# Gates folded into the first stage's tables, and v taken off W's later blocks by VectorE in a chunked delta rule

## The chip, the cores and the metric

One core of one Trainium2 chip runs the whole program. The metric is the device time of one execution in microseconds. The engines are named PE (matmuls; PEld is its weight load), DVE (VectorE), ACT (ScalarE), POOL (GpSimd) and SP (the queue that issues all DMAs here).

## The reference

A layer over x of 4 x 512 tokens and 512 channels, in float32: attention by a gated delta rule, a layer norm, a ternary feed-forward, a layer norm. The change lies in the delta rule, 16 heads of 128 channels:

```
q = silu(conv4(x @ Wq)); k = silu(conv4(x @ Wk)) / sqrt(128); v = silu(conv4(x @ Wv))
a = sigmoid(x @ Wa + ba)          # per head and value channel
beta = sigmoid(x @ Wb + bb)       # per head
for t in range(512):
    err = S @ k_t - v_t
    S   = a_t[:, None] * S - (beta_t * err)[:, None] * k_t[None, :]
    o_t = S @ q_t
```

## The kernel before

The program is a row of stages with barriers between them: projections (pa), recurrence (pb), attention output (pc), preparation of the feed-forward weights (pd), feed-forward (pe).

**Projections.** `projections` goes head by head through 16 heads, with the 128 channels of a head on the partitions and 2048 tokens along the free dimension. PE makes five products a head (A, V, Q, K, G, in four batches each of 12 matmuls, since each operand is split into a high and a low part). Each engine has its own `head`, in a fixed order. DVE: takes A out of PSUM into av, adds one to the exponential ra (so that ra = 1/a), multiplies -ra/128 into ng (ng then holds the gate of the error, -beta/(128 a)), and goes on with the four taps of v (L435 and three times L438), of q, `scaled_v` (v times sqrt(128) times the factors in vt, L414) and the taps of k; between them it makes the low parts of the next head's weights (`split`, L394). ACT: exponential into ra, sigmoid into av, copies of PE's banks to y, the silus. POOL multiplies products of a and 1/a inside blocks of BL = 8 tokens: factors A (inside a block, for the output), vt (to scale v), and r_out with two tables per block, the ratio of one block to the one before it and the running ratio from the chunk's start. Its steps are counted in s_pr, 21 a head. SP stores ng, A, r, vt, q, then loads the weights of the head after next, stores g and k, and loads beta for the next head into ng's buffer. ng's buffer is free for that when the store of ng has landed.

**Recurrence.** `recurrence` goes through 16 chunks of CH = 32 tokens, for 64 pairs of head and batch at once. A chunk has NBL = 4 blocks of 8 tokens; the pairs are worked on in two halves (hf 0 and 1), whose blocks alternate in an order written out by hand in `cycle` of each engine, with the numbers of banks and steps in T_... and D_... tables. PE multiplies the state UT with k and q (`state_products`); DVE's `start` scales the result by the running ratio, the first block into w (in PSUM), the later blocks into W, the q part into O. v is taken off: DVE's `first_v` for the first block, POOL's `less_v` (L778) for W's later blocks. `solve` runs 8 times a chunk: it multiplies w by the gates ng (L1188) into x and solves the block token by token (L1197, L1202). The second half's gates of blocks 2 and 3 come from ngx, a copy by ACT. x goes through ACT and PE (transposes, `cross`), and DVE's `cross` scales PE's result by the block ratio into w and adds the next block of W. POOL also multiplies pair products by the gates (`with_gates`), masks, rescales X (L799) and decays UT by crow (L771).

The lines of the diff, with the line numbers of the profile:

Of the kernel before, what the change touches and what calls it, by code (L numbers as in the profile page):

```python
# [58 lines left out]
def projections(nc, x, w_mats, ba, wb, bb, conv_w, conv_b, scr):  # L59
# [10 lines left out]
    with ExitStack() as ctx:  # L70
# [48 lines left out]
        s_st = {n: m.sem(f"st_{n}") for n in ("q", "k", "ng", "vt", "A", "g", "r")}  # L119
# [11 lines left out]
        N_PR = 21  # L131
# [68 lines left out]
        def _(pool):  # L200
# [13 lines left out]
            def head(h, first):  # L214
# [264 lines left out]
def recurrence(nc, scr, mats, wo, part, res, first):  # L479
# [17 lines left out]
    with ExitStack() as ctx:  # L497
# [238 lines left out]
        def _(pool):  # L736
# [53 lines left out]
            def cycle(c, lower, upper, p, kind):  # L790
# [359 lines left out]
        def _(dve):  # L1150
# [9 lines left out]
            def start(at, p, j, by=1):  # L1160
# [839 lines left out]
```

## Time and profile before

| | |
|---|---|
| median of 3 runs | 2785.17 us (2784.39 to 2795.73) |
| profiled execution | 2792.46 us, span 2790.7 us |
| projections | from the start to about 926 us |
| recurrence | about 932 to 2032 us |
| busy share of the span | PE 92%, PEld 79%, DVE 73%, ACT 43%, POOL 52% |
| mean granted TensorE clock | 0.968 of full speed |

A row of a timeline gives the start, the time to the end of the merged instructions, and in brackets how long the engine was idle before and for whom. A row of a group gives total busy time and the mean of one, then idle time before it by who released it. A row of waits gives total, number and longest. Matmuls are pipelined, so a busy PE need not be at its peak.

### The profile page before, as it was taken

The numbers are of one execution on the slowest core, as the hardware profiler recorded it, in microseconds if no ns is written. First come the engines' busy times: TensorE is split into PE (matmuls) and PEld (weight loads), VectorE is DVE, ScalarE is ACT, GpSimd is POOL, SyncE is SP. The second block draws the span as 40 slices with busy tenths as digits, with TensorE's granted clock in tenths as the row PEclk, the third lists the DMA queues.
The fourth block names the chain that finished last, engine by engine and source line by source line (L and its number), as shares of the span: only waits on it lengthen the run. The fifth ranks groups of instructions, "written<-read, shape, count | busy, mean of one in ns | idle before, by whom it ended". The sixth has DMA issues, their size and how long they took to land. (4 is left out here: it accounts for less than half of the span.)

```text
span 2790.7 us, 50619 instructions
## 1 busy us (share of the span) xinstructions
PE 2578.7 (92%) x17812; PEld 2216.3 (79%) x17922; DVE 2042.4 (73%) x5887; ACT 1204.5 (43%) x2393; POOL 1445.2 (52%) x1216
## 2 busy tenths in 40 slices
PE   8999999999999489999999999999749997899999
PEld 6888888888888378888888888888637776788887
DVE  4776778678769279999999999989768886433333
ACT  4445445544454233333333333323568874433333
POOL 2644553455355489999889898979422220000000
PEclk9999999999999799999999999989859999999999
DMA  5466555655664855555556566555654543100000
GB/s 132 129 177 185 150 146 163 187 143 146 171 179 124 266 201 215 200 198 198 215 227 231 214 230 227 214 197 198 240 202 158 213 188 122 67 12 11 11 11 15
DMA packets 417321, 454.39 MB, mean 163 GB/s; under 512 B 122497, under 2 KB 367233, under 8 KB 393857
## 3 DMA queue, kind: packets, MB, share of 16 engines
q1 hardware_dynamic: 417152, 452.22, 48.6%
q8 instruction: 97, 1.59, 0.2%
q14 instruction: 72, 0.58, 0.1%
HBM read 321.49 MB, written 131.14 MB: 162 GB/s over the span
## 5 line engine op out<-in xcount | busy, mean ns | idle before, releaser
L355 PE MATMUL pa_ps<-pa_x_hi,pa_w_hi 128*128 128x512 f32 x1296 | 507.0, 391 | 9.4 <-ACT pa_y L298 5.2
L355 PE MATMUL pa_ps<-pa_x_lo,pa_w_hi 128*128 128x512 f32 x1296 | 505.1, 390 | 0.0
L355 PE MATMUL pa_ps<-pa_x_hi,pa_w_lo 128*128 128x512 f32 x1296 | 504.9, 390 | 0.0
L438 DVE SCALAR_TENSOR_TENSOR pa_cv<-pa_y,pa_taps,pa_cv 128x2048 f32<-128x2048 f32 x144 | 357.1, 2480 | 17.8
L1197 DVE TENSOR_TENSOR pb_tmp<-pb_gb,pb_ps 128x112 f32<-128x112 f32 (+6 forms) x1792 | 328.5, 221 | 25.5 <-POOL pb_gb L787 11.6
L787 POOL TENSOR_TENSOR pb_gb<-pb_gb,pb_ng 128x448 f32<-128x448 f32 (+6 forms) x448 | 331.6, 786 | 2.9 <-DMA pb_gb<-scratch_pairs 2.9
L1202 DVE TENSOR_TENSOR pb_ps<-pb_ps,pb_tmp 128x112 f32<-128x112 f32 (+6 forms) x1792 | 330.8, 226 | 0.0
L355 PEld LDWEIGHTS pa_ps<-pa_x_hi,pa_w_hi 128*128 128x128 f32 x1296 | 243.6, 188 | 67.1 <-ACT pa_y L298 9.4
L771 POOL TENSOR_TENSOR all_res<-all_res,pb_crow 128x1024 f32<-128x1024 f32 x120 | 281.9, 2367 | 6.1 <-DMA pb_crow<-scratch_crow 6.1
L355 PEld LDWEIGHTS pa_ps<-pa_x_hi,pa_w_lo 128*128 128x128 f32 x1296 | 243.7, 188 | 50.7
L355 PEld LDWEIGHTS pa_ps<-pa_x_lo,pa_w_hi 128*128 128x128 f32 x1296 | 243.6, 188 | 50.0
L1033 PE MATMUL pb_ps<-pb_Gm,pb_XT 128*128 128x64 f32 (+1 forms) x2048 | 249.5, 279 | 10.0 <-DVE all_res L1222 6.3
L1033 PEld LDWEIGHTS pb_ps<-pb_Gm,pb_XT 128*128 128x128 f32 x2048 | 243.7, 197 | 16.0 <-issue 11.2
L225 POOL TENSOR_TENSOR pa_o_vt<-pa_av 128x256 f32<-128x256 f32 x16 | 11.6, 724 | 456.3 <-ACT pa_av L318 456.3
L1008 PE MATMUL pb_ps<-pb_kq,all_res 128*128 128x64 f32 x2048 | 239.6, 277 | 0.0
L1008 PEld LDWEIGHTS pb_ps<-pb_kq,all_res 128*128 128x128 f32 x2048 | 236.5, 195 | 0.7
L1891 DVE SCALAR_TENSOR_TENSOR pe_hid<-pe_ps,all_scales,pe_sil 128x512 f32<-128x512 f32 x64 | 48.1, 751 | 226.6 <-ACT pe_sil L1775 226.6
L851 ACT ACTIVATE pb_XT<-pb_ps 128x512 f32<-128x512 f32 x256 | 140.7, 595 | 137.7 <-PE pb_ps L983 137.5
L983 PEld LDWEIGHTS pb_ps<-pb_ident,pb_X 128*128 128x128 f32 x1024 | 118.5, 145 | 90.7 <-ACT pb_X L879 73.1
L983 PE MATMUL pb_ps<-pb_ident,pb_X 128*128 128x128 f32 x1024 | 144.7, 285 | 42.5 <-ACT pb_X L879 42.0
L1222 DVE TENSOR_TENSOR all_res<-all_res,pb_ps 128x512 f32<-128x512 f32 x240 | 148.7, 681 | 29.5 <-PE pb_ps L1046 29.5
L452 DVE SCALAR_TENSOR_TENSOR pa_o_ng<-pa_ra,pa_o_ng 128x512 f32<-128x512 f32 x64 | 74.5, 1222 | 127.0 <-DMA pa_o_ng<-scratch_beta 127.0
(191 smaller groups left out, 5426.9 us busy)
## 6 DMA issues: line engine op xcount, KB each, us to landing
pb_crow<-scratch_crow SPq DMA_DIRECT2D x30, 2048.0 KB, 10.0
pb_gb<-scratch_pairs SPq DMA_DIRECT2D x64, 896.0 KB, 6.6
pa_o_ng<-scratch_beta SPq DMA_DIRECT2D x16, 1024.0 KB, 7.9
scratch_ng<-pa_o_ng SPq DMA_DIRECT2D x16, 1024.0 KB, 4.5
scratch_A<-pa_o_A SPq DMA_DIRECT2D x16, 1024.0 KB, 4.5
scratch_vt<-pa_o_vt SPq DMA_DIRECT2D x16, 1024.0 KB, 4.5
scratch_q<-pa_o_q SPq DMA_DIRECT2D x16, 1024.0 KB, 6.9
scratch_g<-pa_o_g SPq DMA_DIRECT2D x16, 1024.0 KB, 7.8
```

What stands on the lines that cost most here:

```text
L355: last = nc.tensor.matmul(out, w[:, mat, k, :], xx[:, k, b * S:(b + 1) * S], start=(k == 0 and n == 0), stop=(k == KT - 1 and n == 2))
L438: nc.vector.scalar_tensor_tensor(out=out, in0=yy[:, :, k:k + S], scalar=tap(k), in1=out, op0=ALU.mult, op1=ALU.add).then_inc(s_tap, 1)
L452: last = nc.vector.scalar_tensor_tensor(out=out, in0=tile(ra, b), scalar=-1.0 / DV, in1=out, op0=ALU.mult, op1=ALU.mult)
L771: tt(uu, uu, crow[:, 8 * (e % 4):8 * (e % 4) + 8, :], ALU.mult).then_inc(s_us, 1)
L787: last = tt(pairs, pairs, ng[:, :, BL * n + t + 1:BL * (n + 1)], ALU.mult)
L851: nc.scalar.activation(out, psT[j % 2][:, :].rearrange("p (g k) -> p g k", g=4), ACT.Copy).then_inc(s_te, by)
L983: last = nc.tensor.transpose(bank[:, q * P:(q + 1) * P], src, ident[:, :])
L1008: last = nc.tensor.matmul(bank[:, 64 * q:64 * q + 64].rearrange("p (a t) -> p a t", a=2), UT[:, 8 * j + q, :], kq[p][:, :, 8 * j + q, :], ...
L1033: last = nc.tensor.matmul(bank[:, 64 * q:64 * q + 32 * kinds].rearrange("p (a i t) -> p a i t", i=4, t=BL), XT[:, g, :], Gm[:, g, 0:kinds, ...
L1197: tt(tmp[:, hs, 0:w], gb[n][:, hs, off[t]:off[t] + w], xs[:, qs, t:t + 1].broadcast_to([P, QUART, w]), ALU.mult).then_inc(s_sv, 1)
L1202: tt(xs[:, qs, t + 1:BL], xs[:, qs, t + 1:BL], tmp[:, hs, 0:w], ALU.add).then_inc(done, 1)
L1222: tt(uu, uu, tile(at, D_STATE[r] + i)[:, :].rearrange("p (q v) -> p q v", q=4), ALU.add).then_inc(s_de, 1)
```

## The change

In the projections POOL multiplies three more tables per head: vt gets the factor ng; rg is ng of blocks 1 to 3 times the ratio of the block to the one before; cg is ng times the running ratio, in ng's own buffer, once the store of ng has landed. rg is written to the memory of ra. SP stores rg and cg; the load of the next beta waits for cg's store, and ACT's exponential for rg's store. `scaled_v` waits for POOL's step 18 of now 24.

In the recurrence the gates are thus in the tables: SP loads cg into W itself and rg into its own buffer, for each half (`load_gates`). `start` multiplies by cg, `cross` by rg, `solve` has no product with gates, and ngx goes. The subtraction of v from W's later blocks goes from POOL's `less_v` to DVE's `later_v`, behind `solve(c, 0, hf)`.

```diff
 outs = {n: m.sb(f"o_{n}", [P, NCH, B, CH]) for n in ("q", "k", "ng", "vt", "A", "g")}
+outs["cg"] = outs["ng"]
+outs["rg"] = ra[:, :, :].rearrange("p b s -> p (b s)")[:, 0:TOK * (CH - BL) // CH].rearrange("p (c b t) -> p c b t", c=NCH, b=B)
...
-        N_PR = 21
+        N_PR, N_VT, N_A = 24, 18, 15
...
-                    sp.wait_ge(s_st["ng"], 16 * h)
+                    sp.wait_ge(s_st["cg"], 16 * h)
...
                 store("A")
+                store("rg")
+                store("cg")
...
+                pool.wait_ge(s_ng, h + 1)
+                mul(flat(tI), flat(tI), flat(outs["ng"]), k)
+                assert n[0] == N_VT
                 for j in range(1, NBL):
...
+                scale = lambda i: r_out[:, i, :, :, :].rearrange("p c b n -> p (c b) n").unsqueeze(3).broadcast_to([P, NCH * B, NBL, BL])
+                k = mul(by_block(outs["rg"]), by_block(outs["ng"])[:, :, 1:, :], scale(0)[:, :, 1:, :], k)
+                pool.wait_ge(s_st["ng"], 16 * h + 16)
+                mul(by_block(outs["cg"]), by_block(outs["ng"]), scale(1), k)
...
                     act.wait_ge(s_pr, N_PR * h)
+                    act.wait_ge(s_st["rg"], 16 * h)
...
-                dve.wait_ge(s_pr, N_PR * (h + 1))
+                dve.wait_ge(s_pr, N_PR * h + N_VT)
...
+            def load_gates(c, hf):
+                half = slice(HALF * hf, HALF * (hf + 1))
+                for name, dst in (("cg", W), ("rg", rg)):
+                    src = flat(scr[name][c, :, :, :]).rearrange("p (h t) -> p h t", h=HB)[:, half, :]
+                    sp.dma_start(flat(dst[:, half, :]), flat(src)).then_inc(s_gl[hf], 16)
...
                 if kind != FIRST:
+                    sp.wait_ge(s_wn[1], 6 * c)
+                    load_gates(c, 1)
...
-                sp.wait_ge(s_ngx, c + 1)
-                sp.wait_ge(s_sv, scaled(c, 3, 0))
-                sp.wait_ge(s_sv, scaled(c, 1, 1))
                 load(ng[:, :, :], "ng", c + 1, s_ngl)
+                sp.wait_ge(s_wn[0], 6 * (c + 1))
+                load_gates(c + 1, 0)
...
+            for hf in range(2):
+                load_gates(0, hf)
...
-                less_v(c, at_d - D_CH + D_S[3], 0)
...
-                less_v(c, at_d + D_S[7], 1)
...
-                nc.scalar.activation(ngx[:, :, :], ng[:, HALF:HB, CH // 2:CH], ACT.Copy).then_inc(s_ngx, 1)
...
-                tt(w_of[hf][:, 8 * q:8 * q + 8, :], src[:, :, 0, 0:BL], rr[p][:, 1, hs, 0:1].broadcast_to([P, 8, BL]), ALU.mult)
-                tt(blocks(W[:, hs, :])[:, :, 1:, :], blocks(src[:, :, 0, :])[:, :, 1:, :], cr[:, :, 1:, :], ALU.mult)
+                tt(x_of[hf][:, 8 * q:8 * q + 8, :], src[:, :, 0, 0:BL], W[:, hs, 0:BL], ALU.mult)
+                tt(W[:, hs, BL:], src[:, :, 0, BL:], W[:, hs, BL:], ALU.mult)
...
+            def later_v(at, c, hf):
+                dve.wait_ge(s_de, at + D_S[4 * hf + 3] + 1 + 4)
+                ww = W[:, HALF * hf:HALF * (hf + 1), BL:]
+                tt(ww, ww, vt[:, HALF * hf:HALF * (hf + 1), BL:], ALU.subtract).then_inc(s_wv, 1)
...
-                tt(xs, ws, gates, ALU.mult).then_inc(s_sv, 1)
...
-                    rb = groups(rr[p][:, 0, hs, n + 1:n + 2]).broadcast_to([P, 8, 4, BL])
-                    tt(groups(w_of[hf]), src[:, :, 1, :, :], rb, ALU.mult).then_inc(s_wn[hf], 1)
+                    tt(groups(x_of[hf]), src[:, :, 1, :, :], groups(rg[:, hs, BL * n:BL * (n + 1)]), ALU.mult).then_inc(s_wn[hf], 1)
...
                 solve(c, 0, 0, early=1 if kind == FIRST else 0)
+                later_v(at - D_CH, c, 0)
...
                 solve(c, 0, 1)
+                later_v(at, c, 1)
```

## Rows read from the trace of the kernel before

**Rows 1.** The page, its first part: busy time, share and instructions of each engine.
```profile
PE 2578.7 (92%) x17812; PEld 2216.3 (79%) x17922; DVE 2042.4 (73%) x5887; ACT 1204.5 (43%) x2393; POOL 1445.2 (52%) x1216
```

**Rows 2.** The table of stages: 14 heads of the projections, then 14 chunks of the recurrence.
```profile
core 0: us, PE busy (x) PEld busy (x) DVE busy (x) ACT busy (x) POOL busy (x), PEclk, DMA share, GB/s
109.00:880.00 771.00, 765.79 (x3361) 629.00 (x3360) 583.97 (x420) 376.82 (x435) 381.38 (x294) 1.00 0.57 161
1031.00:1946.00 915.00, 878.29 (x9349) 808.32 (x9446) 831.83 (x4137) 299.99 (x697) 817.61 (x735) 0.99 0.57 212
```

**Rows 3.** The waits of the same 14 heads: us in total, times, longest.
```profile
DVE pa_o_ng L452 <- DMA pa_o_ng<-scratch_beta: 124.6, 14, 9.5
...
DVE pa_ra L447 <- ACT pa_ra L316: 46.2, 14, 3.4
...
PE pa_ps L355 <- ACT pa_y L298: 5.2, 9, 0.8
```

**Rows 4.** The timeline of POOL over one head of the projections.
```profile
606.66 0.70 POOL L225 TENSOR_TENSOR pa_o_vt<-pa_av 128x256 f32<-128x256 f32 x1 [29.64 <-ACT pa_av L318]
...
627.90 4.48 POOL L225 TENSOR_TENSOR pa_r_out<-pa_r_out 128x64 f32<-128x64 f32 x3
632.33 2.44 POOL L256 COPY pa_r_out<-pa_r_out 128x64 f32<-128x64 f32 x1
661.91 0.70 POOL L225 TENSOR_TENSOR pa_o_vt<-pa_av 128x256 f32<-128x256 f32 x1 [27.15 <-ACT pa_av L318]
```

**Rows 5.** The timeline of DVE over the same head.
```profile
613.89 4.44 DVE L452 SCALAR_TENSOR_TENSOR pa_o_ng<-pa_ra,pa_o_ng 128x512 f32<-128x512 f32 x4 [9.36 <-DMA pa_o_ng<-scratch_beta]
...
651.23 1.28 DVE L394 TENSOR_TENSOR pa_w_lo<-pa_w_in,pa_w_hi 128x512 fp32r<-128x512 f32 x2
...
668.44 4.41 DVE L452 SCALAR_TENSOR_TENSOR pa_o_ng<-pa_ra,pa_o_ng 128x512 f32<-128x512 f32 x4 [8.66 <-DMA pa_o_ng<-scratch_beta]
```

**Rows 6.** The timeline of SP's queue over the end of that head.
```profile
652.69 0.40 SPq L161 DMA_DIRECT2D pa_w_in<-in_Wa  x1
...
660.61 2.37 SPq L166 DMA_DIRECT2D pa_o_ng<-scratch_beta  x1
```

**Rows 7.** The timeline of DVE in the recurrence: a gate product, its successor, start tile 7.
```profile
1511.14 0.43 DVE L1188 TENSOR_TENSOR pb_ps<-pb_ps,pb_ng 128x256 f32<-128x256 f32 x1
1511.68 0.45 DVE L1197 TENSOR_TENSOR pb_tmp<-pb_gb,pb_ps 128x112 f32<-128x112 f32 x2
...
1518.43 0.23 DVE L1166 TENSOR_TENSOR pb_ps<-pb_ps,pb_rr 128x64 f32<-128x64 f32 x1 [0.57 <-PE pb_ps L1008]
```

**Rows 8.** Two lines of the attention output: duration ns min/median/max, first and last start us.
```profile
L1402 POOL TENSOR_TENSOR pc_o_in<-pc_o_in,pc_a_in x8: 4494/4613/4787, 2044.5 to 2291.5; 128x2048 f32<-128x2048 f32 x8
...
L1569 DVE TENSOR_TENSOR pc_wo_lo<-all_res,pc_wo_hi x16: 677/684/5021, 2042.5 to 2066.5; 128x512 fp32r<-128x512 f32 x16
```

**Rows 9.** Groups of POOL in the recurrence, shapes kept apart: busy us, mean ns.
```profile
L771 POOL TENSOR_TENSOR all_res<-all_res,pb_crow 128x1024 f32<-128x1024 f32 x112 | 263.2, 2367 | 0.0
...
L778 POOL TENSOR_TENSOR pb_W<-pb_W,first_A 128x768 f32<-128x768 f32 x29 | 52.8, 1821 | 0.0
...
L799 POOL TENSOR_TENSOR pb_X<-pb_X,pb_rr 128x768 f32<-128x768 f32 x29 | 44.5, 1535 | 17.4 <-PE pb_ps L983 17.4
...
L799 POOL TENSOR_TENSOR pb_X<-pb_X,pb_rr 128x256 f32<-128x256 f32 x29 | 19.5, 672 | 64.7 <-PE pb_ps L983 64.7
```

**Rows 10.** Two lines of DVE in the projections, by duration as in rows 8.
```profile
L452 DVE SCALAR_TENSOR_TENSOR pa_o_ng<-pa_ra,pa_o_ng x64: 684/1182/1622, 51.8 to 886.1; 128x512 f32<-128x512 f32 x64
...
L438 DVE SCALAR_TENSOR_TENSOR pa_cv<-pa_y,pa_taps,pa_cv x144: 2350/2352/3106, 61.6 to 921.5; 128x2048 f32<-128x2048 f32 x144
```

**Rows 11.** The table of stages for two short stretches: stores of r, then of vt and q.
```profile
639.20:642.60 3.40, 3.40 (x16) 2.81 (x15) 3.40 (x7) 2.97 (x2) 0.00 (x0) 1.00 0.76 61
645.00:650.00 5.00, 5.00 (x24) 4.14 (x23) 4.72 (x3) 1.71 (x2) 0.00 (x0) 1.00 1.07 324
```

**Rows 12.** The timeline of ACT: the exponential of the head that POOL starts at 661.91.
```profile
656.60 1.92 ACT L316 ACTIVATE pa_ra<-pa_av 128x2048 f32<-128x2048 f32 x1
```

More of the change, by code:

```diff
@@ L118, in projections @@
         s_vt = m.sem("vt")
-        s_st = {n: m.sem(f"st_{n}") for n in ("q", "k", "ng", "vt", "A", "g", "r")}
+        s_st = {n: m.sem(f"st_{n}") for n in ("q", "k", "ng", "vt", "A", "g", "r", "rg", "cg")}
         x_rows = x.rearrange("b (s p) d -> (b s) p d", p=P)
@@ L206, in _ @@
             nc.gpsimd.memset(r_out[:, :, :, :, :], 0.0).then_inc(s_g, 4)
+            flat = lambda t: t[:, :, :, :].rearrange("p c b t -> p (c b t)")
+            by_block = lambda t: t[:, :, :, :].rearrange("p c b (n i) -> p (c b) n i", i=BL)
             at = lambda t, i: t[:, :, :].rearrange("p b (c n i) -> p i b c n", n=NBL, i=BL)[:, i]
@@ L255, in head @@
                     k = mul(rv[:, 1, :, :, j:j + 1], before, rv[:, 0, :, :, j:j + 1], k)
-                step(nc.gpsimd.tensor_copy(rv[:, 1, :, :, 0:1], rv[:, 0, :, :, 0:1]))
+                k = step(nc.gpsimd.tensor_copy(rv[:, 1, :, :, 0:1], rv[:, 0, :, :, 0:1]))
+                scale = lambda i: r_out[:, i, :, :, :].rearrange("p c b n -> p (c b) n").unsqueeze(3).broadcast_to([P, NCH * B, NBL, BL])
+                k = mul(by_block(outs["rg"]), by_block(outs["ng"])[:, :, 1:, :], scale(0)[:, :, 1:, :], k)
+                pool.wait_ge(s_st["ng"], 16 * h + 16)
+                mul(by_block(outs["cg"]), by_block(outs["ng"]), scale(1), k)
                 assert n[0] == N_PR
@@ L513, in recurrence @@
         gb = [m.sb(f"gb{i}", [P, HB, PAIRS]) for i in range(NBL)]
-        ngx = m.sb("ngx", [P, HALF, CH // 2])
+        rg = m.sb("rg", [P, HB, CH - BL])
         tmp = m.sb("tmp", [P, HB, BL - 1])
@@ L519, in recurrence @@
         psT, psD, wx = ps[0:2], ps[2:6], ps[6:8]
-        w_of = [t[:, 0:HALF * BL].rearrange("p (h t) -> p h t", t=BL) for t in wx]
-        x_of = [t[:, HALF * BL:2 * HALF * BL].rearrange("p (h t) -> p h t", t=BL) for t in wx]
+        x_of = [t[:, 0:HALF * BL].rearrange("p (h t) -> p h t", t=BL) for t in wx]
         s_id = m.sem("id")
@@ L546, in recurrence @@
         s_sv = m.sem("sv")
-        s_ngx = m.sem("ngx")
+        s_gl = [m.sem(f"gl{i}") for i in range(2)]
         s_rs = [m.sem(f"rs{i}") for i in range(2)]
@@ L1179, in solve @@
                     dve.wait_ge(s_w, 2 * c + hf + 1)
-                    dve.wait_ge(s_ngl, 16 * (c + 1))
                 else:
                     dve.wait_ge(s_wn[hf], 6 * c + 2 * n)
-                gates = ng[:, HALF * hf:HALF * (hf + 1), BL * n:BL * (n + 1)]
-                if hf and n >= NBL // 2:
-                    dve.wait_ge(s_ngx, c + 1)
-                    gates = ngx[:, :, BL * n - CH // 2:BL * (n + 1) - CH // 2]
-                ws, xs = w_of[hf], x_of[hf]
-                tt(xs, ws, gates, ALU.mult).then_inc(s_sv, 1)
+                xs = x_of[hf]
                 dve.wait_ge(s_m, NBL * c + n + 1)
-                dve.wait_ge(s_sv, 27 * k + 1)
                 quarters = [(q, slice(QUART * q, QUART * (q + 1)), slice(QUART * (2 * hf + q), QUART * (2 * hf + q + 1))) for q in range(2)]
@@ L1195, in solve @@
                         if t:
-                            dve.wait_ge(s_sv, 27 * k + 1 + 4 * (t - 1) + 2 + q + 1)
+                            dve.wait_ge(s_sv, 26 * k + 4 * (t - 1) + 2 + q + 1)
                         tt(tmp[:, hs, 0:w], gb[n][:, hs, off[t]:off[t] + w], xs[:, qs, t:t + 1].broadcast_to([P, QUART, w]),
@@ L1199, in solve @@
                     for q, qs, hs in quarters:
-                        dve.wait_ge(s_sv, 27 * k + 1 + 4 * t + q + 1)
+                        dve.wait_ge(s_sv, 26 * k + 4 * t + q + 1)
                         done = s_sv if w > 1 else s_x[hf]
@@ L1215, in cross @@
                     dve.wait_ge(s_wv, 2 * c + hf + 1)
-                    tt(w_of[hf], w_of[hf], W[:, hs, BL * (n + 1):BL * (n + 2)], ALU.add).then_inc(s_wn[hf], 1)
+                    tt(x_of[hf], x_of[hf], W[:, hs, BL * (n + 1):BL * (n + 2)], ALU.add).then_inc(s_wn[hf], 1)
             def state(at, c, r):
@@ L1238, in cycle @@
                 solve(c, 2, 0)
+                dve.wait_ge(s_gl[1], 32 * (c + 1))
                 for j in range(4, 8):
@@ L1256, in cycle @@
                     dve.wait_ge(s_os[1 - p], 16 * upper + 16 * (1 - p))
+                    dve.wait_ge(s_gl[0], 32 * (c + 2))
                     for j in range(4):
@@ L1261, in _ @@
             dve.wait_ge(s_rl[0], 32)
+            dve.wait_ge(s_gl[0], 32)
             for j in range(4):
@@ L1955, in layer @@
 def layer(nc, x, Wq, Wk, Wv, Wa, ba, Wb, bb, Wg, Wo, cqw, cqb, ckw, ckb, cvw, cvb, ln_w, ln_b, W_up, W_gate, W_down, out):
-    scr = {n: nc.dram_tensor(f"scratch_{n}", (NCH, P, NH, CT), F32, kind="Internal").ap() for n in ("q", "k", "ng", "vt", "A", "g", "o")}
+    scr = {n: nc.dram_tensor(f"scratch_{n}", (NCH, P, NH, CT), F32, kind="Internal").ap() for n in ("q", "k", "ng", "vt", "A", "g", "o", "cg")}
+    scr["rg"] = nc.dram_tensor("scratch_rg", (NCH, P, NH, B * (CH - BL)), F32, kind="Internal").ap()
     scr["beta"] = nc.dram_tensor("scratch_beta", (NH, TOK), F32, kind="Internal").ap()
```

11 lines of the change are left out of this document (1 added, 10 removed).

## Prediction

> **What bounds the kernel now.** I read the page first, then a table of stages, the waits and the timelines of one head and of one chunk. The page gives PE 92% of the span, DVE 73%, POOL 52% [rows 1]. That is an average over stages, and the diff touches two: the projections (16 heads) and the recurrence (16 chunks). In 14 heads PE is busy for 765.8 of 771 us, DVE for 584, POOL for 381; in the recurrence PE for 878 of 915, DVE for 832, POOL for 818 [rows 2].
>
> A first reading of the projections is "PE is full, the rest has room". The waits say something else. DVE never waits for PE there. It waits 124.6 us in 14 heads, 8.9 a head, for beta to land in ng's buffer, and 46.2 for the exponential, while PE waits only 5.2 us for ACT [rows 3]. One head takes 55.25 us by POOL's timeline (606.66 to 661.91) [rows 4]. The same number comes out of a loop without PE: DVE works from 613.89, when beta is there, to the end of the taps of k at 651.23 (37.3 us, where its `split` of G starts), and the next beta is there at 668.44, 17.2 us later [rows 5]; together 54.6. Those 17.2 us are fixed by SP's order: weights at 652.69 (after the split of G), g, k, then beta at 660.61 [rows 6]. PE's 240 products of a head need at most 54.7 us (3361 of them are recorded in 765.8 busy us [rows 2]). So two loops of equal length stand side by side, and whatever lengthens DVE's work between beta and the taps of k lengthens the head in full.
>
> In the recurrence DVE and PE hand over to each other: PE has 2.6 us a chunk left (36.7 over some 14 chunks), DVE still waits for PE in places (0.57 us ahead of a start tile) [rows 2, 7]. POOL is 89% busy, but nobody waits for it there.
>
> **Projections: what POOL gets.** Per head three multiplications are added, all with SBUF on both sides: v's factors by ng (128x2048), rg (128x1536, one operand broadcast), cg (128x2048, one operand broadcast). The first costs 4.6 us: the 128x2048 product of the later stage takes 4613 ns [rows 8]. For a broadcast operand the nearest rows are X by rr: 128x256 672 ns, 128x768 1535 ns, so 1.69 ns an element: 2.8 us for rg, 3.7 us for cg [rows 9]. Sum 11.1 us; at the price without broadcast (2.25 ns an element) it would be 12.7. POOL stands idle for 27 us a head [rows 4], so POOL itself takes them in: 28.1 + 11.1 us of 55.
>
> **What they do to DVE.** This decides. In the projections POOL's work runs against DVE's: a product of 128x64 there is part of a group of 3 that takes 4.48 us, and a copy of 128x64 takes 2.44 us, the length of one DVE tap [rows 4, 10]; DVE's multiplication for ng takes 684 ns at best and 1182 at the median, its taps 2350 and up to 3106 [rows 10]. Each holds the other up for one instruction, so short POOL operations cost DVE little. A long one is seen once: of 16 splits of Wo that take 684 ns at the median, one takes 5021 ns, and it runs while POOL's 4.6 us product does [rows 8]. DVE thus lost 4.34 us to an operation of 4.61, all but 0.3 of it. I take that as the price: each added operation holds DVE up for its own length less 0.3 us. All three come behind ng in POOL's order, so they fall into DVE's stretch of taps, splits and `scaled_v`: POOL's first two r_out products end at 627.9 [rows 4], DVE has work until 651. DVE's idle stretches (beta, exponential) are no refuge, because ng must exist first. So 11.1 - 3 x 0.3 = 10.2 us a head. Bounds: 0, if the one long instance does not carry over, and 12.7 at the dearer product.
>
> The Trainium skill, SBUF — State Buffer, section "Who interferes with whom", states this as a rule: a DVE instruction with two SBUF inputs contends with a GpSimd instruction that reads SBUF, the pair is held for the whole instruction and the loser blocks. By the rule DVE would lose 11.1 us a head instead of 10.2, 14 us more in all; the 5021 ns row agrees with it but for 0.3 us.
>
> **The stores and waits.** SP gets rg and cg (0.75 and 1 MB) behind the wait for POOL's last step, which moves from 634.8 to about 652 in that frame, and with them A, r, v and q move too. `scaled_v` waits only for POOL's step 18, so that is no new stall. The queue then moves A, rg, cg, r, v, q (5 MB) in a row: at 324 GB/s [rows 11], and some 4.5 us for r, whose stretch moves 61 GB/s at 0.76 busy [rows 11], that is 20 us. Weights, g, k and beta queue behind. POOL's end lies 11 to 16 us ahead of DVE's last tap, so the queue is 4 to 8 us in arrears at first; but a later beta lets POOL's short operations run alone and end earlier, which gives part back. I take 2.5 us a head, with bounds 0 and 7. The other new waits cost nothing: ACT's exponential waits for rg's store (landed some 7 us after POOL's end, A and rg at 324 GB/s and a round trip; DVE's last tap alone lies 11 us or more after that end, and without that cover it would cost up to those 7), and beta's load waits for cg's store, which lies far ahead of k in the same queue. Adding it up: 12.7 us a head, x 16 = 203 us.
>
> **Recurrence: what DVE loses and gets.** The multiplication by the gates ahead of each solve goes: start to start 0.54 us (1511.14 to 1511.68) [rows 7], 8 a chunk, 4.3 us. `start` and `cross` keep their instructions with another operand, at the same price. `later_v` adds two subtractions of 128x768 with both inputs in SBUF: 684 ns for 512 columns [rows 8] gives 1.0 us each. They are the only such instructions of DVE there, so they could hit a POOL operation (2.4 us at most, the decay of UT by crow [rows 9]). But they stand right behind each half's first solve, where POOL waits for the transposes of that solve; I take no wait, and 2.4 us each as the bound. Net -2.3 us of DVE a chunk. What of it reaches the end is less: DVE's wait for start tile 7 grows by what solve 2 saves, since PE runs without a gap from the cross product to that tile; the same holds ahead of tile 3. Following the chunk through, each half keeps 0.3 to 0.5 us: 0.8 us a chunk, -13 us over 16; bounds -37 and +38 (both subtractions behind a decay). POOL loses 2 x 1.82 us [rows 9] and ACT the copy of ngx, neither on the path. The gate loads (1.75 MB a chunk) come half a chunk before their use at a busy share of 0.57 [rows 2]; hidden.
>
> **Ends.** After the last head rg and cg are stored behind a later POOL end: +4 us. At the start of the recurrence 1.75 MB more go ahead of the gram writes, 5 us at 350 GB/s, half hidden by PE's wait for POOL's memset: +3 us.
>
> Sum: 203 - 13 + 7 = 197. The profiled execution took 2792.46 us, 7.3 above the median of the runs; against its own time 2989, against the median **2982 us**.
>
> **Rivals.**
> - *Blocked in full and queue in arrears* (the forecast): 2982, alone between 2920 and 3070. Chance 0.66.
> - *POOL's idle 27 us take it all*: long operations do not hold DVE up, heads stay at 55.25, and the recurrence gains. 2785 - 13 + 7 = 2779, and 2755 if the whole -2.3 us a chunk arrives. For it: POOL's large reserve, and a single long instance against it. It decides when the lock costs DVE under 0.4 us a head. 0.10 (half of it below -0.5%).
> - *Half of it*: DVE and POOL fall into a phase in which one or two of the three operations lie in DVE's waits, or only POOL's own loop counts (28 + 11 + three waits for a DVE tap, the store of rg 7 us, exponential and sigmoid 5.3 [rows 4, 12], some 58 us a head). 3 to 7 us a head, 2830 to 2890. 0.16.
> - *The queue dominates*: late weights hold up ACT's splits and so PE too; 18 us a head or more, 3075 and above. 0.08.
>
> About 0.5%, 14 us, can be told from no change. Faster by more 0.05, within 0.06 (the other half of the second case and little of the third), slower 0.89. The range 2850 to 3070 leaves out the second case, a part of the third and the fourth.
>
> **What would show it.** In 14 heads DVE's busy time rises by some 10 us a head while its number of instructions stays; single taps and splits of up to 5 to 7 us appear; POOL's idle time before a head shrinks to about 17 to 27 us while the head takes about 68; PE waits for ACT's copies for some 12 us a head. In the recurrence L1188 is gone, `later_v` takes 1.0 us, the waits of DVE for PE grow. It is wrong if taps stay at 2.35 us beside a 4.6 us product, or if the head's length stays at 55.

## The result, and the profile after

The changed kernel takes 2971.16 us (median of 4 runs, 2969.15 to 2979.24), the kernel before 2787.78 beside it (2784.39 to 2795.73): ratio 1.0659, 95% interval 1.0627 to 1.0691. The forecast was 2982. The profiled execution took 2972.48 us, span 2970.7, mean granted clock 0.941.

The page's busy line, as [rows 1]:

```profile
PE 2624.3 (88%) x17812; PEld 2253.6 (76%) x17922; DVE 2156.1 (73%) x5791; ACT 1197.3 (40%) x2377; POOL 1585.8 (53%) x1232
```

PE fell from 92% to 88%, and no other engine took the lead. The table of stages says where, for some 14 heads and some 14 chunks (us; PE, PEld, DVE, ACT, POOL; clock, DMA share, GB/s), as [rows 2]:

```profile
112.00:1048.00 936.00, 819.49 (x3376) 663.97 (x3375) 709.60 (x424) 382.38 (x438) 552.45 (x336) 0.93 0.59 163
1220.00:2120.00 900.00, 861.03 (x9329) 801.64 (x9425) 807.88 (x4046) 291.29 (x671) 765.09 (x703) 0.99 0.65 243
```

Some fourteen heads take 936 us instead of 771 (the windows do not begin at the same point of a head; counted between loads of beta, below, 14 heads are 937 and 777). POOL's busy time grew by 12.2 us a head ((552.45 - 381.38) / 14), the work it was given. DVE's grew by 9.0 ((709.60 - 583.97) / 14) for nearly the same instructions (424 and 420). Which of them, a view of DVE's groups tells, first of the kernel before over its 14 heads (109 to 880), then of the one after (112 to 1048); total busy us and the mean of one, idle time before it:

```profile
L438 DVE SCALAR_TENSOR_TENSOR pa_cv<-pa_y,pa_taps,pa_cv 128x2048 f32<-128x2048 f32 x126 | 309.2, 2454 | 17.2
L435 DVE TENSOR_SCALAR pa_cv<-pa_y,pa_taps,pa_cbias 128x2048 f32<-128x2048 f32 x42 | 69.1, 1645 | 0.0
...
L394 DVE TENSOR_TENSOR pa_w_lo<-pa_w_in,pa_w_hi 128x512 fp32r<-128x512 f32 x70 | 58.7, 855 | 0.0
...
L414 DVE SCALAR_TENSOR_TENSOR pa_o_vt<-pa_cv,pa_o_vt 128x512 f32<-128x512 f32 x56 | 34.9, 685 | 0.2 <-POOL pa_r_out L256 0.2
```

```profile
L452 DVE SCALAR_TENSOR_TENSOR pa_cv<-pa_y,pa_taps,pa_cv 128x2048 f32<-128x2048 f32 x126 | 339.9, 2698 | 17.2
L449 DVE TENSOR_SCALAR pa_cv<-pa_y,pa_taps,pa_cbias 128x2048 f32<-128x2048 f32 x42 | 117.8, 2804 | 0.0
L408 DVE TENSOR_TENSOR pa_w_lo<-pa_w_in,pa_w_hi 128x512 fp32r<-128x512 f32 x70 | 81.3, 1177 | 0.0
L466 DVE SCALAR_TENSOR_TENSOR pa_o_ng<-pa_ra,pa_o_ng 128x512 f32<-128x512 f32 x56 | 64.7, 1213 | 158.1 <-DMA pa_o_ng<-scratch_beta 158.1
L428 DVE SCALAR_TENSOR_TENSOR pa_o_vt<-pa_cv,pa_o_vt 128x512 f32<-128x512 f32 x56 | 58.1, 1096 | 0.0
```

The counts are equal here and the durations are not: +30.7, +48.7, +22.6 and +23.2 us in these four groups, and -2.2 in ng (66.9 before). That is 123.0 us, 8.8 a head. The wait for beta grew from 124.6 [rows 3] to 158.1, 2.4 a head. Together 11.2, of the 11.4 by which a head is longer (below).

One head shows how an instruction comes to be long. POOL's three products (L231 here), with their neighbours:

```profile
743.85 4.94 POOL L231 TENSOR_TENSOR pa_o_vt<-pa_o_vt,pa_o_ng 128x2048 f32<-128x2048 f32 x1
...
757.56 3.22 POOL L231 TENSOR_TENSOR pa_ra<-pa_o_ng,pa_r_out 128x1536 f32<-128x1536 f32 x1
760.85 4.10 POOL L231 TENSOR_TENSOR pa_o_ng<-pa_o_ng,pa_r_out 128x2048 f32<-128x2048 f32 x1
```

DVE in the same stretch:

```profile
744.23 5.64 DVE L449 TENSOR_SCALAR pa_cv<-pa_y,pa_taps,pa_cbias 128x2048 f32<-128x2048 f32 x1
...
757.94 8.76 DVE L428 SCALAR_TENSOR_TENSOR pa_o_vt<-pa_cv,pa_o_vt 128x512 f32<-128x512 f32 x4
766.63 1.34 DVE L449 TENSOR_SCALAR pa_cv<-pa_y,pa_taps,pa_cbias 128x2048 f32<-128x2048 f32 x1
```

The first tap of q takes 5.64 us beside the 4.9 us product; the first tap of k, with POOL idle, takes 1.34 us (766.63): 4.3 us lost. The four parts of `scaled_v` start 0.4 us behind rg and take 8.76 us, where four take 2.49 with POOL idle: 6.3 us lost to rg and cg (7.3 us). In sum 10.6 of 12.3 us in this head. All three products by duration (min/median/max ns):

```profile
L231 POOL TENSOR_TENSOR pa_o_vt<-pa_o_vt,pa_o_ng x16: 4612/4930/6627, 87.3 to 1070.5; 128x2048 f32<-128x2048 f32 x16
L231 POOL TENSOR_TENSOR pa_ra<-pa_o_ng,pa_r_out x16: 3199/3216/5024, 94.6 to 1085.6; 128x1536 f32<-128x1536 f32 x16
L231 POOL TENSOR_TENSOR pa_o_ng<-pa_o_ng,pa_r_out x16: 4067/4622/5736, 98.0 to 1088.9; 128x2048 f32<-128x2048 f32 x16
```

At their shortest they take 4.6, 3.2 and 4.1 us. The up to 2 us more I read as POOL waiting out an instruction of DVE first.

**Two loops take turns.** Two successive heads of DVE, from ng to ng:

```profile
663.97 5.06 DVE L466 SCALAR_TENSOR_TENSOR pa_o_ng<-pa_ra,pa_o_ng 128x512 f32<-128x512 f32 x4 [12.77 <-DMA pa_o_ng<-scratch_beta]
...
727.03 4.55 DVE L466 SCALAR_TENSOR_TENSOR pa_o_ng<-pa_ra,pa_o_ng 128x512 f32<-128x512 f32 x4 [8.49 <-DMA pa_o_ng<-scratch_beta]
...
797.00 4.78 DVE L466 SCALAR_TENSOR_TENSOR pa_o_ng<-pa_ra,pa_o_ng 128x512 f32<-128x512 f32 x4 [13.03 <-DMA pa_o_ng<-scratch_beta]
```

The first takes 63.1 us: 45.6 to the split of G (709.58), at which SP has been waiting, and 17.4 to the next ng, the 17.2 of before. The second takes 70.0 us. There POOL's last product ends at 764.95, and SP's queue runs from there to the next beta:

```profile
764.98 0.37 SPq L172 DMA_DIRECT2D scratch_A<-pa_o_A  x1
...
788.77 2.25 SPq L168 DMA_DIRECT2D pa_o_ng<-scratch_beta  x1
```

Between these two it goes from one transfer to the next without a wait (A, rg, cg, r, v, q, weights, g, k, beta): 37.9 us from ng to POOL's end, 32.0 from there to the next ng. SP's own waits for DVE's split count the heads of the first kind:

```profile
SPq L163 <- DVE pa_w_lo L408: 46.9, 7, 6.8
```

7 of 14; before it was 13 of 13 in such a window, 100.8 us. In the first head ng comes late, so POOL's short products run while DVE stands idle (POOL waits 0.70 us for ng), and POOL ends 26.9 us behind ng; beta then comes earlier, the short products run against DVE's, and POOL ends late in the next.

The three products cost DVE the same in both kinds. In the first head the 4.90 us product starts at 669.19, rg at 682.88, cg at 686.18, and DVE beside them:

```profile
669.56 5.62 DVE L449 TENSOR_SCALAR pa_cv<-pa_y,pa_taps,pa_cbias 128x2048 f32<-128x2048 f32 x1
...
683.27 3.91 DVE L449 TENSOR_SCALAR pa_cv<-pa_y,pa_taps,pa_cbias 128x2048 f32<-128x2048 f32 x1
687.32 10.61 DVE L452 SCALAR_TENSOR_TENSOR pa_cv<-pa_y,pa_taps,pa_cv 128x2048 f32<-128x2048 f32 x3
```

A first tap takes 1.34 us and three taps 7.33 with POOL idle, so 4.3, 2.6 and 3.3 us are lost, 10.1 in all, against 10.6 in the second kind. What is missing to that in the group sums (8.8 a head) is what POOL's short products cost DVE behind ng before the change, 2.6 us in the head of [rows 5] (a split of 1.19 us, a first tap of 2.15, three taps of 8.39): in the heads of the first kind they are through before ng. From ng to the split of G DVE takes 37.3 us before [rows 5], 45.6 in the first kind and 48.3 in the second.

**The sum over the program**, from starts of instructions in both traces. Loads of beta, first to last of 16: 42.1 to 875.0 before (55.5 us a head), and after:

```profile
L168 SPq DMA_DIRECT2D pa_o_ng<-scratch_beta x16: 506/2292/2954, 44.2 to 1048.5; - x16
```

That is 66.95 a head, +11.4, +171.4 over 15 heads. POOL starts the recurrence at 932.7 before and 1118.3 after, +185.6: 171.4, 2.1 ahead of the first load, 12.1 between the last load and the recurrence (57.7 us became 69.8: the sixteenth head). From there to the first solve 38.2 us became 44.0 (+5.8). From the first to the last step of the solves 1054.2 became 1039.6 (-14.6). Behind it +3.1. Sum: 185.6 + 5.8 - 14.6 + 3.1 = 179.9, and the spans differ by 180.0.

### The profile page after: what moved, and what is told of

Read it like the earlier page. It is cut to its first block and busy times, and to the rows that moved or that the text cites. A ratio compares the mean times of both kernels' runs of the same rounds, so it can differ in the third digit from the quotient of the medians.

```text
span 2970.7 us, 50611 instructions
## 1 busy us (share of the span) xinstructions
PE 2624.3 (88%) x17812; PEld 2253.6 (76%) x17922; DVE 2156.1 (73%) x5791; ACT 1197.3 (40%) x2377; POOL 1585.8 (53%) x1232
## 5 line engine op out<-in xcount | busy, mean ns | idle before, releaser
L369 PE MATMUL pa_ps<-pa_x_hi,pa_w_hi 128*128 128x512 f32 x1296 | 529.7, 409 | 123.6 <-ACT pa_y L311 56.8
L369 PE MATMUL pa_ps<-pa_x_lo,pa_w_hi 128*128 128x512 f32 x1296 | 523.6, 404 | 0.0
L369 PE MATMUL pa_ps<-pa_x_hi,pa_w_lo 128*128 128x512 f32 x1296 | 522.3, 403 | 0.0
L452 DVE SCALAR_TENSOR_TENSOR pa_cv<-pa_y,pa_taps,pa_cv 128x2048 f32<-128x2048 f32 x144 | 389.8, 2707 | 17.9
L369 PEld LDWEIGHTS pa_ps<-pa_x_hi,pa_w_hi 128*128 128x128 f32 x1296 | 255.8, 197 | 191.9 <-ACT pa_y L311 61.5
L369 PEld LDWEIGHTS pa_ps<-pa_x_hi,pa_w_lo 128*128 128x128 f32 x1296 | 254.8, 197 | 55.6
L369 PEld LDWEIGHTS pa_ps<-pa_x_lo,pa_w_hi 128*128 128x128 f32 x1296 | 256.0, 198 | 53.6
L231 POOL TENSOR_TENSOR pa_o_vt<-pa_av 128x256 f32<-128x256 f32 x16 | 11.6, 725 | 429.8 <-ACT pa_av L332 429.8
L814 POOL TENSOR_TENSOR pb_X<-pb_X,pb_rr 128x256 f32<-128x256 f32 (+2 forms) x96 | 106.2, 1106 | 153.4 <-PE pb_ps L992 153.3
L1228 DVE TENSOR_TENSOR all_res<-all_res,pb_ps 128x512 f32<-128x512 f32 x240 | 148.6, 680 | 43.1 <-PE pb_ps L1055 43.0
```

Source lines behind the costliest of these rows:

```text
L369: last = nc.tensor.matmul(out, w[:, mat, k, :], xx[:, k, b * S:(b + 1) * S], start=(k == 0 and n == 0), stop=(k == KT - 1 and n == 2))
L452: nc.vector.scalar_tensor_tensor(out=out, in0=yy[:, :, k:k + S], scalar=tap(k), in1=out, op0=ALU.mult, op1=ALU.add).then_inc(s_tap, 1)
L1228: tt(uu, uu, tile(at, D_STATE[r] + i)[:, :].rearrange("p (q v) -> p q v", q=4), ALU.add).then_inc(s_de, 1)
```

## The experiments

Eleven kernels ran, on several chips, each beside the kernel before (medians of before 2792.26 to 2794.02 there). "Head" is the distance between loads of beta, (last - first) / 15.

**The products alone.** The kernel before with POOL's three products, without their stores, and with the recurrence of before. The stored vt then holds one factor too many, so the output is another one.

```diff
+                mul(flat(tI), flat(tI), flat(outs["ng"]), k)
...
+                k = mul(by_block(outs["rg"]), by_block(outs["ng"])[:, :, 1:, :], scale(0)[:, :, 1:, :], k)
+                pool.wait_ge(s_st["ng"], 16 * h + 16)
+                mul(by_block(outs["ng"]), by_block(outs["ng"]), scale(1), k)
```

> The kernel before with only POOL's three added products in the projections (results left in vt, ra's memory and ng; v is thus scaled by ng too, so the output is not the reference's), without the added stores, gate loads and waits, and with the recurrence of before. Theory A (DVE is held up by POOL's long products): DVE's busy time rises by 8 to 9 us a head, the head goes from 55.5 to 64 to 66 us, total 2925 to 2955 us. Theory B (the added stores and the waits on them lengthen the head, the products fit POOL's 27 idle us): heads stay at 55.5, total 2785 to 2800.

Measured: 2957.33 us, just above the range of theory A, ratio 1.0579 (1.0551 to 1.0606). Head 65.7 us, +10.2. DVE's wait for beta:

```profile
DVE pa_o_ng L462 <- DMA pa_o_ng<-scratch_beta: 130.6, 14, 12.4
```

That is 9.3 us a head (8.9 before), and SP waits for DVE's split in 13 of 13 heads, 61.6 us: DVE's loop sets every head here. Nine tenths of the loss (164 of 183 us) come with the products alone, and nearly all of that is DVE's longer instructions: its taps, first taps, splits, `scaled_v` and ng, equal in number, take 139.8 us more over 14 heads, 10.0 a head. All heads are of one kind here, with some 48 us from ng to the split of G.

**The stores alone.** The kernel before with the two stores and their waits; what they write is nobody's input.

```diff
-                    sp.wait_ge(s_st["ng"], 16 * h)
+                    sp.wait_ge(s_st["cg"], 16 * h)
...
+                store("rg")
+                store("cg")
```

> The kernel before with only the added stores and waits: rg and cg are stored from ra's memory and ng's buffer, the exponential waits for rg's store and beta's load for cg's store; no product, recurrence of before (the two stored tables are not read). Theory A: POOL ends as early as before, so the 1.75 MB more are through before the weights are due: 0 to 1 us a head and some 5 us at the end of the projections, total 2790 to 2810. Theory B: this is where the 11.4 us a head come from, total 2930 to 2970.

Measured: 2800.91 us, ratio 1.0022 (1.0008 to 1.0036). Head 55.9 us, +0.3; the recurrence starts 10 us later, about half of it behind the last head. 1.75 MB more a head in a queue that has room cost nearly nothing. Behind late products they cost 1.2 us a head (66.95 - 65.7).

**POOL busy, but only writing.** The kernel after with the products replaced by memsets of 128x2048, four in all (the first line below stands in a loop of three); stores, waits and recurrence are those of after, the tables hold constants.

```diff
-                mul(flat(tI), flat(tI), flat(outs["ng"]), k)
...
+                    k = step(nc.gpsimd.memset(flat(ra4), 0.0))
+                step(nc.gpsimd.memset(flat(outs["cg"]), 0.01))
...
-                k = mul(by_block(outs["rg"]), by_block(outs["ng"])[:, :, 1:, :], scale(0)[:, :, 1:, :], k)
...
-                mul(by_block(outs["cg"]), by_block(outs["ng"]), scale(1), k)
```

> The changed kernel with POOL's three products replaced by four memsets of 128x2048 (1.8 us each by the memset of O, 7.2 us a head) among the small r_out products; rg and cg then hold constants and v lacks the factor ng, so the output is not the reference's. If POOL holds DVE up only by an instruction that reads SBUF against a DVE instruction with two SBUF inputs: taps with two inputs stay at 2350 ns at the median and never above 3.2 us, total 2785 to 2820. If every long POOL instruction holds DVE up: 7.2 less 4 x 0.3 = 6 us a head, total 2875 to 2900.

Measured: 2827.15 us, ratio 1.0108 (1.0085 to 1.0132), a little above the range expected. Head 58.0 us. DVE's taps and first taps by duration:

```profile
L452 DVE SCALAR_TENSOR_TENSOR pa_cv<-pa_y,pa_taps,pa_cv x144: 2350/2352/3111, 64.9 to 958.0; 128x2048 f32<-128x2048 f32 x144
L449 DVE TENSOR_SCALAR pa_cv<-pa_y,pa_taps,pa_cbias x48: 1333/2148/3076, 62.6 to 950.8; 128x2048 f32<-128x2048 f32 x48
```

One head, POOL's memsets and DVE beside them:

```profile
659.78 1.81 POOL L266 MEMSET pa_ra<- 128x2048 f32 x1
...
662.89 1.82 POOL L266 MEMSET pa_ra<- 128x2048 f32 x1
664.64 1.81 POOL L267 MEMSET pa_o_ng<- 128x2048 f32 x1
```

```profile
660.30 2.37 DVE L449 TENSOR_SCALAR pa_cv<-pa_y,pa_taps,pa_cbias 128x2048 f32<-128x2048 f32 x1
662.80 7.32 DVE L452 SCALAR_TENSOR_TENSOR pa_cv<-pa_y,pa_taps,pa_cv 128x2048 f32<-128x2048 f32 x3
```

The taps, with two inputs in SBUF, keep their length beside two memsets (three in 7.32 us, and 7.33 with POOL idle; maximum 3111 ns, 3106 in [rows 10]). The first tap, with one SBUF input of 2048, does not: 2.37 us here for 1.34, median 1456 to 2148 ns (1456 is that of the run with the stores alone), about 1 us a head. `scaled_v` shows nothing: in this head it starts at 670.64, behind POOL's last instruction (667.80). The rest of the 2.5 us is beta, because POOL ends later. The Trainium skill, SBUF — State Buffer, section "Who interferes with whom", says both: a DVE instruction with two SBUF inputs contends with a GpSimd instruction that reads, not with one that only writes, and a `tensor_scalar` can take both ports in its fast mode and then contends too. This run agrees, with three taps in 7.32 us and a first tap of 2.37.

**In quarters.** The kernel after with each product cut in four, so that no POOL instruction is longer than a tap.

```diff
-                mul(flat(tI), flat(tI), flat(outs["ng"]), k)
+                for q in range(4):
+                    part = slice(TOK // 4 * q, TOK // 4 * (q + 1))
+                    mul(flat(tI)[:, part], flat(tI)[:, part], flat(outs["ng"])[:, part], k)
```

> The changed kernel with each of the three products cut into four pieces (12 instructions, same elements, same results). Theory A with a price of own length less 0.3 us an instruction: pieces of about 1.2, 0.9 and 1.1 us, 12.8 us together, less 12 x 0.3: DVE loses 9.2 us a head as in the changed kernel, POOL ends later because every piece waits for a DVE instruction of up to 2.35 us, total 2965 to 3020. Rival: short pieces slip in between DVE's instructions, as the small r_out products seem to, DVE loses 3 us or less a head, total 2860 to 2900.

Measured: 2997.13 us, ratio 1.0727 (1.0693 to 1.0761), head 68.6. One head's products, and DVE's ng:

```profile
752.84 10.40 POOL L231 TENSOR_TENSOR pa_o_vt<-pa_o_vt,pa_o_ng 128x512 f32<-128x512 f32 x4 [3.36 <-DVE pa_o_ng L472]
...
770.16 8.40 POOL L231 TENSOR_TENSOR pa_ra<-pa_o_ng,pa_r_out 128x384 f32<-128x384 f32 x4
778.64 6.43 POOL L231 TENSOR_TENSOR pa_o_ng<-pa_o_ng,pa_r_out 128x512 f32<-128x512 f32 x4
```

```profile
750.18 2.50 DVE L472 SCALAR_TENSOR_TENSOR pa_o_ng<-pa_ra,pa_o_ng 128x512 f32<-128x512 f32 x4 [16.80 <-DMA pa_o_ng<-scratch_beta]
```

The products take 25.2 us instead of 12.3; I read the difference as pieces that wait for an instruction of DVE. DVE's stretch is shorter: from ng to the split of G 41.9 us (750.18 to 792.12), where 14 heads after take 43.1 to 48.3 (mean 46.6) and one before 37.3 [rows 5]. But its instructions beside the pieces still take 8.9 us more than with POOL idle: the first taps of v and k 2.32 and 2.11 us (1.34), the taps 9.73, 7.71 and 7.93 for three (7.33), a split 1.35 (0.68), `scaled_v` 5.61 (2.49). The gain is elsewhere: ng comes so late that POOL's short products are through, and ng itself takes 2.50 us instead of 4.44. SP never waits for a split of DVE in this run: POOL ends 34.9 us behind ng (785.07) in every head, the next ng comes 32.1 us later (817.16), and DVE waits 16.8 us. So theory A's 9.2 us for DVE is met (8.9), and its total too, but what sets each head, 67.0 us, is now POOL's end and the queue.

**The products on DVE.** The kernel after with the three products moved to DVE, ahead of `scaled_v`.

```diff
+                nc.vector.tensor_tensor(flat(outs["vt"]), flat(outs["vt"]), flat(outs["ng"]), ALU.mult).then_inc(s_vt, 1)
+                nc.vector.tensor_tensor(by_block(outs["rg"]), by_block(outs["ng"])[:, :, 1:, :], scale(0)[:, :, 1:, :], ALU.mult).then_inc(s_vt, 1)
+                nc.vector.tensor_tensor(by_block(outs["cg"]), by_block(outs["ng"]), scale(1), ALU.mult).then_inc(s_vt, 1)
```

> The changed kernel with the three products done by DVE, ahead of scaled_v, instead of POOL; same results. By the rows of a 128x512 product (684 ns) and a 128x2048 one (2288 ns) they cost DVE 2.3 + 1.75 + 2.3 = 6.3 us a head and hold nobody up. Theory A: head of 55.5 + 6.4 and 0 to 3 us for stores that come late, 62 to 65 us, total 2880 to 2935, so less than the 8.8 us that the same work on POOL takes from DVE. If DVE were not part of the loop that sets the head, it would be 2785 to 2800.

Measured: 2897.28 us, ratio 1.0379 (1.0348 to 1.041), head 62.3. DVE needs 2.29 + 1.75 + 2.29 = 6.3 us for what costs it 8.8 while POOL does it. The engine that is on the path does the work more cheaply than the idle one next door.

**Beta earlier, in both kernels.** Beta for the next head is loaded right behind the store that frees its buffer, ahead of weights, g and k. First in the kernel after:

```diff
+                if left:
+                    sp.wait_ge(s_st["cg"], 16 * h + 16)
+                    load_beta(h + 1)
```

> The changed kernel with SP's load of the next head's beta moved from behind k's store to right behind q's store (it still waits for cg's store to land); same results. Theory A (loop of DVE and SP): DVE no longer waits 8 to 11 us a head for beta, the loop is DVE's own: 8.6 us from the end of the taps of k to ng plus 48 to 51, so 57 to 60 us a head instead of 66.95, total 2830 to 2880. If PE or POOL set the head, nothing changes: 2965 to 2975.

Measured: 2947.91 us, ratio 1.0547 (1.0514 to 1.0579). Head 64.95: 2.0 us less than after, where 7 to 10 were expected. The waits of 14 heads:

```profile
DVE pa_o_ng L471 <- DMA pa_o_ng<-scratch_beta: 78.9, 14, 7.6
...
ACT pa_w_hi L288 <- DMA pa_w_in<-in_Wa: 65.2, 14, 6.7
```

SP's queue in one head, which begins when POOL ends:

```profile
679.63 0.37 SPq L174 DMA_DIRECT2D scratch_A<-pa_o_A  x1
...
693.00 2.82 SPq L166 DMA_DIRECT2D pa_o_ng<-scratch_beta  x1
696.11 0.39 SPq L163 DMA_DIRECT2D pa_w_in<-in_Wa  x1
```

Half of the wait for beta is gone (158 to 79), and ACT waits for the weights instead. SP waits for no split of DVE in this run: the second loop (POOL's late end, seven stores, beta, weights, the next head) sets all of them. That theory's simple form, that only the place of beta matters, fell here. The same edit in the kernel before, with `s_st["ng"]`:

> The kernel before with the same move of beta's load to right behind q's store. Theory A: DVE's loop falls to some 47 to 50 us, so PE's 54.4 to 54.7 us a head are the bound: 0.5 to 1 us a head less than the 55.5 of before, total 2770 to 2782, and DVE waits for PE at the taking out of A. Rival (PE is the bound already): 2785 to 2790.

Measured: 2782.26 us, ratio 0.9962 (0.9948 to 0.9977), head 54.3: 0.4% less than the kernel before. SP and DVE:

```profile
639.12 2.39 SPq L164 DMA_DIRECT2D pa_o_ng<-scratch_beta  x1
643.49 0.40 SPq L161 DMA_DIRECT2D pa_w_in<-in_Wa  x1
```

```profile
651.94 2.50 DVE L457 SCALAR_TENSOR_TENSOR pa_o_ng<-pa_ra,pa_o_ng 128x512 f32<-128x512 f32 x4
```

The wait of 8.66 us [rows 5] is gone, and the head is only 1.3 us shorter: ng follows ng at 54.40 us in 13 heads, and PE is busy for all of the 751.00 us from 109 to 860. The other loop, PE's 240 products of at most 54.7 us [rows 2], is the floor. The two loops of equal length in the prediction are shown by this.

**The move of v's subtraction, by itself.** In the kernel after, `less_v` back on POOL:

```diff
+                less_v(c, at_d - D_CH + D_S[3], 0)
...
-                later_v(at - D_CH, c, 0)
```

> The changed kernel with the subtraction of v from W's later blocks back on POOL, where less_v stood; gates stay folded, same results. It takes 1.9 us a chunk off DVE, of which PE's stretches swallow about half: 0 to 1 us a chunk, total 2955 to 2971. Rival (POOL's relief of 3.6 us a chunk is what the recurrence gained by): the recurrence gets 10 us or more slower, 2981 and above.

Measured: 2963.64 us, ratio 1.0613 (1.0592 to 1.0634). Over the kernel before run beside it that is 171 us, some 12 less than after (183); the intervals of the two ratios touch. From the first to the last step of the solves it is 1027.2 us (1039.6 after). In the kernel before, `later_v` on DVE:

> The kernel before with only less_v moved to DVE as later_v, behind each half's first solve; gates not folded, same results. DVE gets 1.9 us a chunk more; with about half of it kept 0.5 to 1.9 us a chunk, total 2793 to 2815. Rival (POOL's relief is what counts): 2775 or less.

Measured: 2804.69 us, ratio 1.0043 (1.0029 to 1.0058); 1058.5 us for the solves (1054.2 before).

```profile
L1169 DVE TENSOR_TENSOR pb_W<-pb_W,first_A x32: 949/951/1141, 977.7 to 1992.9; 128x768 f32<-128x768 f32 x32
```

One trace each is not much: the same recurrence takes 1044.9 to 1054.2 us (mean 1050.2) in the four traces that keep that of before, and 1032.2 to 1045.6 (mean 1037.6) in the seven that keep that of after. Both new traces lie outside, 1058.5 above the four and 1027.2 below the seven, so the sign holds. Against the means the two subtractions cost 0.5 and 0.65 us a chunk; by the medians of the whole kernels it is 12 us both times, 0.8 a chunk, for two instructions of 0.95. This half of the change costs, folding the gates gains (1050.2 or 1054.2 to 1027.2, 1.4 to 1.7 us a chunk), and no gain from POOL's relief is seen.

**Can the folded gates be made to pay?** Products on DVE and beta early, together:

```diff
+                    sp.wait_ge(s_st["cg"], 16 * h + 16)
+                    load_beta(h + 1)
...
+                nc.vector.tensor_tensor(by_block(outs["cg"]), by_block(outs["ng"]), scale(1), ALU.mult).then_inc(s_vt, 1)
```

> The kernel after with two changes of the projections: the three products on DVE (65.7 us a head between loads became 62.3 there), and beta of the next head issued right behind the store of cg instead of at the head of the next head's queue. Theory A (what sets a head is DVE's chain and the wait for beta behind it, and with the products on DVE, ng, rg and cg are ready at one time, early in the head, so the stores are not late as they were when GpSimd made them): the wait of DVE for beta shrinks from 139 us in 14 heads to under 60, a head takes 55 to 58 us instead of 62.3, PE's 54.4 us is the floor, the whole 2775 to 2830. Theory B (the queue of stores and loads is a loop of its own also here: 1.75 MB more a head ahead of the weights and beta, as when beta alone was moved in the kernel after and gained 2.0 us a head): 59 to 62 us a head and 2850 to 2895, with ACT waiting for the weights. Rival (the folded gates beat the kernel before once GpSimd is out of it): under 2775.

Measured: 2861.09 us, ratio 1.0244 (1.0226 to 1.0263), head 59.7. Both are numbers of theory B, but not by its mechanism. DVE waits 3.8 us for beta in all and ACT not at all for weights. The new wait stands in DVE:

```profile
677.26 1.19 DVE L408 TENSOR_TENSOR pa_w_lo<-pa_w_in,pa_w_hi 128x512 fp32r<-128x512 f32 x1
683.65 2.29 DVE L429 TENSOR_TENSOR pa_o_vt<-pa_o_vt,pa_o_ng 128x2048 f32<-128x2048 f32 x1 [5.20 <-POOL pa_r_out L269]
```

DVE has come round to `scaled_v` before POOL's small products of r are ready, and the taps of k stand behind that wait. So they were put ahead of it:

```diff
+                taps_of(K)
                 scaled_v(h)
-                taps_of(K)
```

> The kernel of the run before (products on DVE, beta early; 59.7 us a head, 2861) with the taps of k moved ahead of the products and of scaled_v in DVE's order. There DVE waited 81.4 us in 15 heads for GpSimd's r_out, 5.4 a head, with the taps of k behind that wait. Theory A (this wait is what the head is now longer than DVE's work and PE's 54.4 us): it goes, since 8.7 us of taps lie in it, and a head takes 55 to 57 us, the whole 2785 to 2820. Theory B (the queue: the stores of A, rg, cg, then beta and the weights come 5 to 8 us later than before in the head, so DVE waits for beta, or ACT for the weights, by as much): 59 to 62 us a head, 2850 to 2900. Rival (folded gates beat the kernel before): under 2778.

Measured: 2896.3 us, ratio 1.0357 (1.0343 to 1.0371), head 62.2, slower than without the move. The wait for POOL is gone, and the queue, which now gets rg and cg at 659.3, after the taps of k, answers:

```profile
DVE pa_o_ng L475 <- DMA pa_o_ng<-scratch_beta: 143.9, 15, 10.7
...
ACT pa_w_hi L283 <- DMA pa_w_in<-in_Wa: 119.6, 14, 9.4
```

Theory B, with a head just above its 62. The best form found with the gates folded is 2.4% slower than before. Of its 68.8 us, heads of 59.7 instead of 55.5 make 62.5.

Not tried: rg and cg in buffers of their own, with the products put into DVE's idle stretches (exponential and beta), which needs room in SBUF beside those of the projections.

## Why the prediction was right, step by step

- **Two loops of equal length.** Right. With beta early in the kernel before, DVE's loop drops away and the head stays at PE's 54.3 us; any lengthening of DVE's stretch lengthens the head in full: +10.2 us from the products alone.
- **Each product holds DVE up for its length less 0.3 us.** Right in kind: 5.64 us for a tap of 1.34. Forecast 10.2 us a head; measured 10.0 with the products alone, 10.1 and 10.6 in the two heads shown, and 8.8 over the kernel before in the groups of after, where in half of the heads POOL's short products no longer fall on DVE. The 10.2 owes something to luck, since two errors offset each other. The products are longer than estimated, 11.9 us instead of 11.1 (rg 3.2 instead of 2.8, cg 4.1 instead of 3.7, so the price per element of the small shapes was too low). And DVE loses less of each: the 4.9 us product costs it 4.3, all but 0.6. The 0.3 was also misread: the product that ran beside the split of 5021 ns is the longest of [rows 8], 4787 ns and not 4613, which leaves 0.45.
- **Late beta and queue, 2.5 us a head.** Measured 2.4 more wait (158.1 against 124.6). With the stores alone it is 0.4 (130.7 us over 14 heads); it takes POOL's late end as well. The giving back that the prediction named is seen in the two kinds of head, 63.1 and 70.0 us.
- **Heads in sum.** Forecast 16 x 12.7 + 4 = 207 us to the start of the recurrence, measured 185.6. The difference is 1.3 us a head.
- **Recurrence.** -13 forecast, -14.6 measured (-12.6 between the means of all traces), and the waits of DVE for PE grew as said, from 63 us over 915 to 85 over 900. `later_v` takes 0.95 us, forecast 1.0, with no wait at the median. Split by the two runs above it is -23 to -27 for the gates and +8 to +12 for v; the net was right, its parts were not priced apart.
- **Start of the recurrence.** +3 forecast, +5.8 measured: four gate loads now stand ahead of the gram writes in SP's queue.
- **PE.** Idle 8.3 us a head ((936 - 819.49) / 14), not some 12, and only 4.1 of it for ACT's copies (56.8 us in 14 heads). Its busy time grew by the other 3.8 us, 58.5 us a head instead of 54.7, at a mean granted clock of 0.93 instead of 1.00 in this stretch.
- **The rivals.** "POOL's idle 27 us take it all" would need taps at 2.35 us beside a 4.6 us product; they are not. "Half of it" asked for 3 to 7 us a head and got 11.4; the two kinds of head are such a change of phase, but even the shorter is 7.6 us over the 55.5 of before. "The queue dominates" was nearer than its chance of 0.08 says: the queue sets half the heads, at 70 us and not at the 73 of that rival, and all of them in quarters and with beta early. Its mechanism, late weights, is not what is seen in after: ACT waits for them once, 4.0 us; it is beta that comes late.

## What to carry to other kernels

An engine's idle time is not free room if a neighbour on the critical loop pays for it: before moving work to it, look for one row where the two already overlap (here one split of 5021 ns beside a product of 4787) and price the neighbour, not the engine. Then write down each loop that closes a turn, with the stores that stand ahead of the next load, since a late producer comes back through the queue, and each loop that is cut uncovers the next (beta, weights, r, beta again). Test the parts of a change apart: here one part gained 1.4 to 1.7 us a chunk, the other gave some of it back, and the place that paid for both was another stage.

## What the runs showed of the hardware that was not expected

- Cutting POOL's products in four doubled their total (12.3 to 25.2 us), a piece of 128x512 of the first going from 1.3 us at best to 2.6 (10.40 / 4), while the taps beside it went from 2.44 to 3.24 (7.33 / 3 and 9.73 / 3). Cutting did not free DVE: it still lost 8.9 us to the pieces, and POOL now lost 12.9 on top.
- The difference between reading and only writing: three taps beside two memsets of POOL took 7.32 us (7.33 with POOL idle), while the first taps, with one SBUF input, went from 1456 to 2148 ns at the median.
- The mean granted clock was 0.93 over the projections of after, with PE idle for 8.3 us a head, 0.97 with products on DVE and beta early (some 4.5 idle a head), and 1.00 in the kernel before [rows 2] and with beta early there, with PE idle for under half a microsecond a head. At 0.93 PE's busy time is 3.8 us a head more. Whether it lengthened any head was not tried; neither of the two loops that set the heads of after goes through PE.
